# Delta rule: inverse halves and updates head by head on quadrants of TensorE, k by rows from VectorE's transposes and ScalarE's block copies, u's decay from a second eviction

## The reference

```python
q, k, v = causal_dwconv(x @ Wq.T), causal_dwconv(x @ Wk.T), causal_dwconv(x @ Wv.T)
g, beta = log_sigmoid(x @ Wg.T), sigmoid(x @ Wb.T)
k = k / norm(k); q = q * Kd ** (-0.5)
def step(S, inp):                      # over the tokens, per head; S is 64 x 64
    Sk = einsum('bhkv,bhk->bhv', S, k_t)
    delta = einsum('bhv,bhk->bhkv', v_t, k_t) - einsum('bhv,bhk->bhkv', Sk, k_t)
    S = exp(g_t) * S + b_t * delta
    o_t = einsum('bhkv,bhk->bhv', S, q_t)
return o.reshape(b, t, H * Kd) @ Wo.T
```

## Time and profile before

| | us |
|---|---|
| median of 3 runs | 4411.03 (4410.61 to 4418.47) |
| profiled execution | 4403.65 |
| its span | 4401.8 |
| granted TensorE clock, mean | 0.975 |

### The profile page before, as it was taken

How to read it: one execution, slowest core, us unless ns; L and a number is a source line. 1 busy time by engine, 2 the same in 40 slices (tenths; PEclk the granted TensorE clock), 3 DMA queues, 4 the chain that set the end, 5 groups by cost and what they waited for, 6 DMA issues and landing times. The chain is left out here.

```text
span 4401.8 us, 115094 instructions
## 1 busy us (share of the span) xinstructions
PE 4160.9 (95%) x45581; PEld 2616.3 (59%) x45581; DVE 3069.3 (70%) x5127; ACT 2350.5 (53%) x3581; POOL 1041.0 (24%) x1045
## 2 busy tenths in 40 slices
PE   5999699999999999999688899999999999999998
PEld 4444399999999999968466244444444444444443
DVE  4899755555555555534698788787878787878886
ACT  2888644544445445415344266565656565656654
POOL 1000154544444454400576400000000000000000
PEclk9999899999999999999899699999999999999999
DMA  3543522222222222124443300000000000000000
GB/s 125 179 124 118 173 79 69 75 84 67 76 80 72 76 78 75 46 69 147 119 110 97 77 9 9 14 10 14 4 18 5 19 5 19 5 8 14 10 14 10
DMA packets 271755, 264.48 MB, mean 60 GB/s; under 512 B 53760, under 2 KB 232064, under 8 KB 270496
## 3 DMA queue, kind: packets, MB, share of 16 engines
q1 hardware_dynamic: 250768, 226.07, 17.1%
q0 software_dynamic: 6144, 16.79, 1.2%
q10 hardware_dynamic: 14352, 14.55, 1.0%
HBM read 151.95 MB, written 105.38 MB: 58 GB/s over the span
## 5 line engine op out<-in xcount | busy, mean ns | idle before, releaser
L2438 DVE TENSOR_REDUCE part_max<-p_m 128x1 f32<-128x512 f32 x2118 | 1363.0, 685 | 378.9 <-PE p_m L2280 371.4
L2420 ACT ACTIVATE prob<-p_s 128x1024 f32<-128x1024 f32 x1024 | 1047.7, 1023 | 749.0 <-PE p_s L2344 746.9
L2299 PE MATMUL p_o<-prob,v_one 128*64 128x512 f32 x4096 | 1055.7, 593 | 3.9 <-ACT prob L2420 0.5
L2280 PE MATMUL p_m<-keys,queries 96*64 96x512 f16 x4236 | 662.0, 387 | 27.9 <-DMA keys<-parts_d 20.3
L2344 PE MATMUL p_s<-queries,keys 97*64 97x512 f16 x4096 | 619.7, 380 | 0.0
L901 PE MATMUL pd_pre<-inv_low,upper_wide 128*128 128x64 f32 x5120 | 614.3, 278 | 2.6 <-DVE inv_low L1272 2.1
L901 PEld LDWEIGHTS pd_pre<-inv_low,upper_wide 128*128 128x128 f32 x5120 | 589.4, 193 | 20.6 <-issue 14.1
L2344 PEld LDWEIGHTS p_s<-queries,keys 97*64 97x64 f16 x4096 | 229.3, 109 | 597.7 <-issue 592.3
L1267 DVE TENSOR_TENSOR step<-pd_pre,const 128x512 f32<-128x512 f32 x320 | 221.2, 691 | 309.5 <-PE pd_pre L901 309.5
L2248 POOL TENSOR_TENSOR attn<-o_num,o_inv 32x512 f32<-32x512 f32 x64 | 81.1, 1267 | 1453.6 <-DVE o_inv L2457 1447.1
L2280 PEld LDWEIGHTS p_m<-keys,queries 96*64 96x64 f16 x4236 | 239.2, 108 | 309.9 <-DVE part_max L2438 56.4
(11 more groups left out here) (239 smaller groups left out, 5874.9 us busy)
## 6 DMA issues: line engine op xcount, KB each, us to landing
q_d<-conv_q SPq DMA_DIRECT2D x16, 1024.0 KB, 5.0
v_d<-conv_v SPq DMA_DIRECT2D x16, 1024.0 KB, 5.0
k_d<-conv_k SPq DMA_DIRECT2D x16, 1024.0 KB, 6.5
sums<-sums_d SPq DMA_DIRECT2D x128, 128.0 KB, 3.1
kq_t<-k_d SPq DMA_DIRECT2D x32, 512.0 KB, 3.8
kq_t<-q_d SPq DMA_DIRECT2D x32, 512.0 KB, 4.9
sums_k<-sums_d SPq DMA_DIRECT2D x128, 128.0 KB
v_t<-v_d SPq DMA_DIRECT2D x32, 512.0 KB, 4.7
```

What stands on the lines that cost most here:

```text
L2280: last = te.matmul(p_m[k % 2][x * HALF:(x + 1) * HALF, :], queries[0:ROW, p, hh, at:at + HALF], keys[0:ROW, 2 * p + hh, kb * BLK:(kb + 1) ...
L2299: product = te.matmul(p_o[64 * hh:64 * hh + VW, :], g.v_one[:, j, p, hh:hh + 2, :].rearrange("p a d -> p (a d)"), prob[:, j % 2, hh, :], s ...
L2420: a.activation(prob[:, j % 2], p_s[j % 2][:], ACT.Exp, scale=SCORE_SCALE).then_inc(exp_d, 1)
L2438: v.tensor_reduce(part_max[:, hh * SUB + sub, kb:kb + 1], p_m[k % 2][:], AX.X, ALU.max).then_inc(red_d, 1)
```

## The change

In words:

- `half` and `updates` become 16 products each, head by head, in the SAME quadrants. `upper_wide` and `widen` are gone; `inv_fin` shrinks to 128x512 and is filled by one copy. `upper` becomes a ring of four tiles. Three POOL memsets at the start of the phase are gone.
- `key_rows` and `take_rows` are gone. `turn_keys` (VectorE, a 128x512 transpose straight from `k_t`) and `keep_rows` (ScalarE, eight 32x256 block copies for each chunk) take their place. `k_row` no longer holds the decay.
- The decay is put on u: `take_updates` evicts `p_u` twice, first into `u_dec` (times `beta_end`), then into `u` (times beta) as before. `new_state` reads `u_dec`. `end_beta` on POOL makes `beta_end` (128x8), two for each couple.

The diff, cut to its core:

```diff
-    upper = [sb(f"upper{x}", W) for x in range(2)]
-    upper_wide = sb("upper_wide", [P, 2, NPAIR, 2 * C])
+    upper = sb("upper", [P, 4, NPAIR, C])
...
-    inv_fin = [sb(f"inv_fin{x}", [P, NPAIR, 2 * C]) for x in range(2)]
+    inv_fin = [sb(f"inv_fin{x}", W) for x in range(2)]
...
         def half(n, x):
-            for p in range(NPAIR):
-                last = te.matmul(p_pre[x][:, p, :], upper_wide[:, x, p, :], inv_low[x][:, p, :], start=True, stop=True)
-            return last
+            return lambda p, h: product(p, h, p_pre[x], SAME, of(upper, n.ring[x]), of(inv_low[x]))
...
         def updates(n, x):
-            for p in range(NPAIR):
-                last = te.matmul(p_u[:, p, :], inv_fin[x][:, p, :], resid[:, p, :], start=True, stop=True)
-            return last
+            return lambda p, h: product(p, h, p_u, SAME, of(inv_fin[x]), of(resid))
...
-            pe.wait_ge(u_d, n.ended[x])
+            pe.wait_ge(udec_d, n.ended[x])
...
-            return lambda p, h: product(p, h, p_n, OTHER, of(k_row, x), of(u))
+            return lambda p, h: product(p, h, p_n, OTHER, of(k_row, x), of(u_dec))
...
-                raised, turned = over_heads(up(pre, 0, 4), key_rows(pre, 0))
-                raised.then_inc(upmm_d[0], 1)
-                turned.then_inc(kr_d[0], 1)
+                over_heads(up(pre, 0, 4))[0].then_inc(upmm_d[0], 1)
...
+        def keep_rows(n, x, h):
+            if h == 0:
+                if n.c > 0:
+                    act.wait_ge(new_d, n.previous[x])
+                act.wait_ge(kt_d[x], n.now)
+            for from_p, from_t, to_p, to_t in blocks_of(h):
+                last = a.activation(k_row[to_p, x, :, to_t], k_turned[from_p, :, from_t], ACT.Copy)
+            if h == 1:
+                last.then_inc(rows_d[x], 1)
...
-            for h in range(2):
-                last = a.activation(inv_fin[x][half_of(h), :, half_of(h)], p_low[x][half_of(h)], ACT.Copy)
-            last.then_inc(up_d[x], 1)
+            a.activation(inv_fin[x][:], p_low[x][:], ACT.Copy).then_inc(up_d[x], 1)
...
+        def turn_keys(n, x):
+            dve.wait_ge(k_in[n.odd], n.filled)
+            if x == 1:
+                dve.wait_ge(rows_d[0], n.now)
+            elif n.c > 0:
+                dve.wait_ge(rows_d[1], n.last)
+            v.transpose(k_turned[:], k_t[:, n.odd, :, x, :]).then_inc(kt_d[x], 1)
...
             dve.wait_ge(new_d, n.begun[x])
+            dve.wait_ge(end_d[x], n.now)
+            dve.wait_ge(w_d, n.ended[x])
+            v.tensor_tensor(u_dec[:], p_u[:], spread(beta_end[:, n.ring[x], :].unsqueeze(2), W), ALU.mult).then_inc(udec_d, 1)
             dve.wait_ge(o_d, n.begun[x])
...
+        def end_beta(n, x):
+            if n.c > 1:
+                pool.wait_ge(udec_d, n.older[x])
+            pool.wait_ge(rel_d[x], n.now)
+            po.tensor_tensor(beta_end[:, n.ring[x], :], rel[:, n.ring[x], :, C], g.beta[:, bass.ds(n.chunk[x], 1), :].rearrange("p a n -> p (a n)"),
+                             ALU.mult).then_inc(end_d[x], 1)
```

More of the change, by code:

```diff
@@ L742, in phase_delta @@
     wo_in, cleared = sem("wo_in"), sem("cleared")
-    old_d, res_d, ress_d, w_d, u_d, o_d, ocp_d = (sem(s) for s in ("old", "res", "ress", "w", "u", "o", "ocp"))
+    udec_d, old_d, res_d, ress_d, w_d, u_d, o_d, ocp_d = (sem(s) for s in ("udec", "old", "res", "ress", "w", "u", "o", "ocp"))
     new_d, sdec_d, state_d = (sem(s) for s in ("new", "sdec", "state"))
@@ L746, in phase_delta @@
     diff_d, min_d, grow_d, rel_d, relb_d, qg_d, kg_d = (sem2(s) for s in ("diff", "min", "grow", "rel", "relb", "qg", "kg"))
-    kq_d, kr_d, rows_d, upper_d, minus_d, wide_d, att_d, inv1_d, vt_d, val_d = (
-        sem2(s) for s in ("kq", "kr", "rows", "upper", "minus", "wide", "att", "inv1", "vt", "val"))
+    kq_d, kt_d, end_d, rows_d, upper_d, minus_d, att_d, inv1_d, vt_d, val_d = (
+        sem2(s) for s in ("kq", "kt", "end", "rows", "upper", "minus", "att", "inv1", "vt", "val"))
     half_d, step_d, lowc_d, upmm_d, up_d = (sem2(s) for s in ("half", "step", "lowc", "upmm", "up"))
@@ L821, in one @@
                 for x in range(2):
-                    sp.wait_ge(kr_d[x], ahead.before)
+                    sp.wait_ge(kt_d[x], ahead.before)
                     sp.wait_ge(kg_d[x], ahead.before)
@@ L929, in wait_old @@
             pe.wait_ge(state_d, n.ended[x])
-            if x == 0:
-                pe.wait_ge(rows_d[1], n.now)
-            else:
-                pe.wait_ge(ocp_d, n.begun[1])
+            pe.wait_ge(ocp_d, n.begun[x])
         def old_outputs(n, x):
@@ L992, in halves @@
             wait_half(n, x, k)
-            half(n, x).then_inc(half_d[x], 1)
+            over_heads(half(n, x))[0].then_inc(half_d[x], 1)
         def one(post, pre, ahead):
@@ L1104, in one @@
             if pre is not None:
-                wait_up(pre, 0, 5)
-                wait_key_rows(pre, 1)
-                raised, turned = over_heads(up(pre, 0, 5), key_rows(pre, 1))
-                raised.then_inc(upmm_d[0], 1)
-                turned.then_inc(kr_d[1], 1)
-                wait_up(pre, 1, 5)
-                over_heads(up(pre, 1, 5))[0].then_inc(upmm_d[1], 1)
+                for x in range(2):
+                    wait_up(pre, x, 5)
+                    over_heads(up(pre, x, 5))[0].then_inc(upmm_d[x], 1)
         pe.wait_ge(g.const_in, 16)
@@ L1142, in keep_values @@
                 last.then_inc(val_d[x], 1)
-        def widen(n, x):
-            if n.c > 0:
-                act.wait_ge(half_d[x], n.level[0])
-            act.wait_ge(minus_d[x], n.now)
-            for h in range(2):
-                last = a.activation(upper_wide[half_of(h), x, :, half_of(h)], upper[x][half_of(h)], ACT.Copy)
-            last.then_inc(wide_d[x], 1)
+        def keep_rows(n, x, h):
[7 more added lines that the diff above has]
+                last.then_inc(rows_d[x], 1)
         def keep_inverse(n, x, k):
@@ L1184, in one @@
                     keep_inverse(pre, x, 2)
+            if pre is not None:
+                keep_rows(pre, 0, 0)
             if post is not None:
@@ L1187, in one @@
             if pre is not None:
+                keep_rows(pre, 0, 1)
                 keep_inverse(pre, 0, 3)
@@ L1198, in one @@
                 keep_values(pre, 1, 1)
-            if ahead is not None:
-                for x in range(2):
-                    widen(ahead, x)
+                keep_rows(pre, 1, 0)
+                keep_rows(pre, 1, 1)
             if post is not None:
@@ L1297, in one @@
             if pre is not None:
+                turn_keys(pre, 0)
                 turn_low(pre, 1, 2)
@@ L1318, in one @@
                 turn_low(pre, 0, 4)
-                take_rows(pre, 0)
                 turn_values(pre, 1)
@@ L1330, in one @@
             if pre is not None:
-                take_rows(pre, 1)
+                turn_keys(pre, 1)
             if ahead is not None:
@@ L1341, in _ @@
         po.memset(rel[:], 0.0).then_inc(cleared, 1)
-        po.memset(upper_wide[:], 0.0).then_inc(cleared, 1)
-        for x in range(2):
-            po.memset(inv_fin[x][:], 0.0).then_inc(cleared, 1)
         pool.wait_ge(cleared, 2)
@@ L1415, in one @@
                 grow_queries(pre, 0)
+                for x in range(2):
+                    end_beta(pre, x)
             if ahead is not None:
```

47 lines of the change are left out of this document (16 added, 31 removed).

## The result

| | before | after |
|---|---|---|
| median of 4 runs, us | 4412.45 | 4261.50 (4256.16 to 4268.16) |
| profiled execution, us | 4403.65 | 4262.45 |
| its span, us | 4401.8 | 4260.7 |
| granted TensorE clock, mean | 0.975 | 0.967 |

The ratio is 0.9656, with a 95% interval of 0.9639 to 0.9673: 151 us faster by the medians, 141 us by the two profiled executions. The forecast was 268 us. The measured time lies 118.5 us above the forecast and 11.5 us above the range. The sign was right, the size was not.

A forecast was written before the change was run, and what follows sets the result against it. TensorE was taken to bound the delta rule; 31 turns x 8.4 us (41.6 to 33.2) = 260, plus 6 and 2, make 268 us off 4403.65: 4136, plus 7.4 for the median, 4143 us. Range 4090 to 4250.

The forecast's parts named there:

- the range: Whole kernel: 4090 to 4250 us, from the case without a new wait to the falling clock.
- The sign: Whole kernel: the change makes it faster, by over 0.2% (9 us) with chance 0.90.
- TensorE bounds the kernel, and its savings are won: Delta rule: TensorE 98% busy, a turn lasts as long as its 26 batches; savings count until another engine is late.
- 12 batches, 0.86 us less each: Halves and updates as quadrant batches take 0.95 us instead of 1.81, saving 10.3 us of each turn.
- The bank: Rival: two heads of halves in one PSUM bank hinder each other, 1.81 us as before; 4411 us, chance 0.04.
- The walk and its wait for `o_t`: One delta rule turn timed batch by batch: TensorE newly waits 1.6 us for ScalarE's copy; next turn at 32.6 us.
- 0.6 us for the irregular gaps: Added to the turn's 32.6 us for gaps of the mean turn over the cleanest (41.6 - 40.98), giving 33.2 us.
- Instructions arrive too slowly: Rival: TensorE's queue brings a packet per 5.73 us, a turn needs 8.3: 47.6 us a turn, 4597 us; chance 0.06.
- its threshold: The instruction queue decides against the change once packets cannot come closer than 41.6 / 8.3 = 5.0 us.
- The rival's sign: Late instructions on TensorE would make the kernel slower than before: 6.0 us a turn, 186 us; chance 0.06.
- The granted clock: Rival: TensorE's clock falls once each turn at the new wait, 3.4 us each, 105 us more: 4248 us; chance 0.20.
- Outside the steady turns: Delta rule ends: 6 us saved in the turn with `pre` alone, 2 us in the last turn.

The follow-up runs named there:

- few_records: The changed kernel with each batch of halves made of 8 products of 128 columns instead of 16 of 64 (inverse partly wrong); 4221.2 us, ratio 0.9571.
- wide3: The changed kernel with the two level 3 batches of halves streaming 128 columns per product instead of 64, same number of instructions; 4249.2 us, ratio 0.9635.
- rows_late: The changed kernel with ScalarE's first eight block copies (k of chunk 0) moved behind both `o_t` copies; 4276.5 us, ratio 0.9692.
- few_45: The changed kernel with only the halves of levels 4 and 5 as 8 products of 128 columns instead of 16 of 64; 4263.0 us, ratio 0.9661.
- few_late: few_records with ScalarE's first eight block copies moved behind both `o_t` copies; 4197.3 us, ratio 0.9507.
- dense_block: The changed kernel plus four wait-free TensorE blocks of 1024 constant products ahead of the delta rule, the second using four quadrants by turns; 4554.8 us, one run.

## Why the prediction was wrong, point by point

- **TensorE bounds the kernel, and its savings are won.** Right for before. After, it no longer holds as "a turn lasts as long as its 26 batches": 86% busy, with no other engine late.
- **12 batches, 0.86 us less each.** The duration was right where instructions are in time: 2.12 us for two batches with their last record's overlap, 64 records.
- **The bank.** Two heads of halves into one tile don't hinder each other. The rule of the Trainium skill ("TensorEngine Tiling (Array Packing)", Restrictions and Gotchas), that different row tiles cannot access one PSUM bank at once, would have made these batches 1.9 us; the trace has 0.95.
- **The walk and its wait for `o_t`.** The mechanism was right and stands in `few_records` with 2.1 us for the 1.6 forecast. In the changed kernel it comes to 0.35 us, since stops of 3.5 us ahead of it give ScalarE the time.
- **"0.6 us for the irregular gaps".** This is the term of the sum that failed. In its place stand 3.5 us at the 256-record step, 1.15 with the indirect DMAs and up to 1.3 by the clock.
- **The rejected rival, "Instructions arrive too slowly", and its threshold.** This is the step that failed. I priced the queue by the pace that it had been asked for, 5.73 us, and tested it against the mean of a turn: "as soon as packets cannot come closer than 41.6 / 8.3 = 5.0 us". They do come closer, 3.7 us apart, so by that test there was no danger. The trace of the kernel before shows the pace too: the closest of its packets start 3.5 to 3.7 us apart, and it has 12.1 us of stops at the 256-record step. The test was wrong because it spread the demand over the turn. The walk itself held what was needed: in the dense stretch, from 5.5 to 17.8, stand 960 records, 3.75 packets, which at 3.7 to 4.0 us each is an estimate of 13.9 to 15.0 us. Its batches there take 10.65 us without the wait. The 3.2 to 4.4 us between are more than the wait for `o_t`, so they contain it; with the stops of the indirect DMAs added, that estimate is 15.0 to 16.2 us, and 15.8 was measured. The rival's sign was wrong too: it was told as an all-or-nothing case on the side of "slower", where a shortage in one stretch only eats part of a gain.
- **The granted clock.** It was priced at 3.4 us in every turn, or nothing. It fell in 19 stretches in 31 turns, and costs 1.3 us a turn at most. The Trainium skill's pattern of HAM oscillation ("TensorE: Matmul & The Clock Gate", HAM oscillation), recurring waits that make the clock fall again, is borne out in kind, as falls now come again and again where the earlier trace rows was alone, but not in every turn. The forecast tied them to the wait for `o_t`, and here mostly the stops stand in its place. The time at half clock is longest in the two kernels that wait most for `o_t` (157.0 us with 62.2 of waiting, 133.1 with 39.5). Among the others it doesn't follow that wait: 34.1 with none in `wide3`, 85.3 with none in `rows_late`, 102.4 with 9.7 in `few_45`. No run held the clock up, so its price isn't measured by itself.
- **Outside the steady turns.** Near enough: the part with `pre` alone gave 11.4 us where I took 6, the part with `post` alone 3.0 where I took 2, and the rest of the program took as long as before. The first mark, which moved by 7.6 us, stands behind the first turn and not behind the part with `pre` alone.
- **The range.** It reached to 4250 by the clock alone. A partial clock and a partial supply shortage together weren't among the cases, and the chance of 0.06 for the queue came from a price that ruled it out too easily.

No version with all of the changed kernel's computation ran measurably faster than it: `wide3`, with 4249.2 us, overlaps it.

## What to carry to other kernels

When a change cuts an engine's work into more and shorter instructions, count the instructions of each dense stretch, not of the whole loop, and hold them against the fastest pace at which the instruction queue has ever been seen to deliver, measured by a block of back-to-back instructions if the trace has none. A stretch at that pace hides what stands in it: removing work, waits or a disturbance there brings nothing, and the extra work of `wide3` cost nothing, until the number of instructions falls. Then the next wait behind it shows, as in `few_records`, and behind that one the next, as in `few_late`.

## What the runs showed of the hardware

- TensorE's instruction queue delivered 256 records (MATMUL, LDWEIGHTS and waits for semaphores) in one packet of 16 KB. Stops at steps in a row were 3.4 us apart at the least and 4.0 in the median in the delta rule, and steps 3.8 us apart on the mean in a block without any other traffic. TensorE went on 2.2 to 3.2 us after a packet's start.
- Four quadrants by turns, in f32 with 64 columns, go through the array at 128 MATMUL records in about 1.9 us, so that a packet left up to 1.9 us idle of 4.00. Streams of 32 columns in two quadrants weren't faster than those of 64: 60.4 us for 1024 products, and 3.9 us for 256 records at 64 columns.
- While GpSimd issued an indirect DMA, dense batches of TensorE stopped every 0.73 us for some 0.4 us of idle time, 65 times in 58 issues. Behind 52 issues in the kernel before, where a whole-array batch stands ahead, that happened at most once.
- In `few_late`, where that issue began 0.1 to 0.5 us behind TensorE's last record of old outputs, TensorE's wait for the semaphore of that batch ended 0.5 to 3.0 us after the record, against 0.5 to 0.6 us in the median in the kernels before and after and in `few_records`. That the issue is the cause was not tested.
- The granted clock fell to 0.50 in the second block of `dense_block` too, whose mean is 0.89 at 38.38 of 60.80 us busy, with no wait for any engine.
